# Inverse roots from an exponential of the bits, and new orders on four engines, in the third stage of a decoder kernel

## The reference

```python
x = attn_layer(shift_tokens(x), ...) + x      # second half of the features comes from the token before
x = ffn_layer(shift_tokens(x), ...) + x

# attn_layer: 16 heads of 64
q, k, v = split(x @ Wqkv)
q = l2norm(q) * qs;  k = l2norm(k) * ksc      # l2norm(t) = t / max(norm(t), 1e-12)
q, k = rotary(q), rotary(k)
out = softmax(mask(8 * q @ k.T)) @ v          # keys from 32 tokens back to the token itself
return out @ Wo
# ffn_layer
xn = (x - mean) / sqrt(var + 1e-05) * g + b
a, gate = split(xn @ W1 + b1)
return a * gelu(gate) @ W2 + b2
```

## Time and profile before

| | before |
|---|---|
| median of 3 runs | 3703.31 us |
| the profiled execution's own time | 3706.61 us |
| span of its trace | 3704.8 us |
| PE busy | 3253.5 us, 88% of the span |
| DVE busy | 2801.0 us, 76% |
| ACT busy | 2487.4 us, 67% |
| POOL busy | 2652.6 us, 72% |
| mean granted TensorE clock | 0.986 of full speed |

### The profile page before, as it was taken

How to read it: one execution, slowest core, us unless ns; L and a number is a source line. 1 busy time by engine, 2 the same in 40 slices (tenths; PEclk the granted TensorE clock), 3 DMA queues, 4 the chain that set the end, 5 groups by cost and what they waited for, 6 DMA issues and landing times.

```text
span 3704.8 us, 124977 instructions
## 1 busy us (share of the span) xinstructions
PE 3253.5 (88%) x51333; PEld 2530.0 (68%) x51333; DVE 2801.0 (76%) x5681; ACT 2487.4 (67%) x4952; POOL 2652.6 (72%) x5005
## 2 busy tenths in 40 slices
PE   8999997888888888888888888888888888888886
PEld 6778775666666666666666666766666666666665
DVE  6844446888787888887888878788778878888885
ACT  5756664676666767666667667677666766667664
POOL 5522227877787887787778877777777778777774
PEclk9999999999999999999999999999999999999999
DMA  4000004444445444444444444444444444444442
GB/s 96 3 8 8 8 6 96 102 95 94 87 103 109 92 93 90 100 104 97 94 93 89 101 104 97 90 93 95 103 103 94 95 88 98 94 98 90 97 95 52
DMA packets 280546, 310.50 MB, mean 84 GB/s; under 512 B 154281, under 2 KB 225582, under 8 KB 279982
## 3 DMA queue, kind: packets, MB, share of 16 engines
q0 software_dynamic: 58368, 201.36, 28.0%
q1 hardware_dynamic: 220892, 100.93, 10.7%
q10 hardware_dynamic: 722, 0.21, 0.0%
HBM read 23.63 MB, written 2.10 MB: 7 GB/s over the span
## 4 chain that ended last, share of the span: by engine, by line
PE 59%; DVE 25%; issue 8%; ACT 5%; POOL 1%; SPq 1%; DMA 1%; DVEq 0%; POOLq 0%
PE bank L1153 10%; PE bank L1235 8%; PE bank L1209 8%; PE bank L1123 8%; DVE RK L1403 6%; DVE Z L1459 6%; PE bank L1094 6%; DVE ss L1424 6%; PE bank L1110 4%; PE bank L1134 3%; ACT sq L1300 3%; ACT xnT L1283 2%; PE bank L709 2%; PE bank L722 2%; PE bank L731 2%
## 5 line engine op out<-in xcount | busy, mean ns | idle before, releaser
L1403 DVE TENSOR_TENSOR RK<-bank,tables 128x1024 f32<-128x1024 f32 x384 | 468.7, 1222 | 329.3 <-ACT sq L1300 326.2
L1209 PE MATMUL bank<-xnT,W 128*128 128x128 f32 (+1 forms) x2304 | 322.8, 294 | 350.0 <-DVE Y L1376 349.3
L1389 DVE TENSOR_TENSOR RQ<-bank,q_tables 128x1024 f32<-128x1024 f32 x384 | 452.1, 1219 | 153.3 <-ACT sq L1294 153.2
L1209 PEld LDWEIGHTS bank<-xnT,W 128*128 128x128 f32 (+1 forms) x2304 | 282.6, 190 | 371.0 <-issue 371.0
L1546 POOL TENSOR_TENSOR P<-P,inv_sum 128x512 f32<-128x512 f32 x384 | 505.7, 1634 | 5.7 <-DVE inv_sum L1471 5.7
L1534 POOL TENSOR_TENSOR RK<-RK,rn 128x512 f32<-128x512 f32 x384 | 400.2, 1042 | 28.4 <-POOL rn L1574 0.9
L1520 POOL DMA_DIRECT2D RQ<-RQ x384 | 350.1, 1041 | 97.2 <-DVE RQ L1389 90.2
L1153 PE MATMUL bank<-WA,xcT 128*128 128x512 f32 x768 | 376.8, 613 | 37.0 <-DVE P L1450 16.7
L1540 POOL TENSOR_TENSOR P<-P,rn 128x512 f32<-128x512 f32 x384 | 402.4, 1048 | 3.8 <-DVE P L1450 3.8
L1267 ACT ACTIVATE kT<-bank 128x512 f32<-128x512 f32 x384 | 229.5, 598 | 249.8 <-PE bank L1094 249.8
L1235 PE MATMUL bank<-WO,OT 128*128 128x128 f32 x3072 | 382.3, 278 | 0.0
(11 more groups left out here) (166 smaller groups left out, 7567.4 us busy)
## 6 DMA issues: line engine op xcount, KB each, us to landing
RQ<-RQ POOLq DMA_DIRECT2D x384, 256.0 KB, 4.0
RK<-RK POOLq DMA_DIRECT2D x192, 512.0 KB, 4.7
Z<-Z SPq DMA_DIRECT2D x768, 64.0 KB, 2.5
WA<-in_wqkv SPq DMA_DIRECT2D x24, 256.0 KB, 2.8
ystat<-Y SPq DMA_DIRECT2D x192, 32.0 KB
ystat<-Y SPq DMA_DIRECT2D x384, 15.8 KB
ys<-Y SPq DMA_DIRECT2D x192, 32.0 KB
ys<-Y SPq DMA_DIRECT2D x384, 15.8 KB
```

Of the source, the lines that this page charges most:

```text
L1209: last = mm(FF_BANK[c][0:rows, side * 128:(side + 1) * 128], m.W1[:, off + at:off + at + rows], m.xnT[:, t % 2, :], start=True, stop=True)
L1389: tt(both, src.unsqueeze(1).to_broadcast([128, 2, 8, SEQ]), m.q_tables[:, layer(t), :, :].unsqueeze(2).to_broadcast([128, 2, 8, SEQ]), ALU ...
L1403: tt(both, src.unsqueeze(1).to_broadcast([128, 2, 16, 32]), tab.unsqueeze(2).to_broadcast([128, 2, 16, 32]), ALU.mult).then_inc(s.rotated. ...
```

## The change

The parts of the diff that only rename or resize semaphores and buffers are left out. A column for the variance is added to ssm, seed and rn (32 to 33 wide), so that the seed and the Newton steps work on 33 numbers for a token. The guess comes from one ACT instruction, an exponential of the float's bits read as an integer; two Newton steps follow in place of three, the first with its constants multiplied by 1 + 1.67e-4. The input of the feed-forward part, ys, gets a third buffer. The orders of ACT, DVE, POOL and SP change; PE keeps its order and gets two other waits.

```diff
+SEED_SCALE = -0.5 * math.log(2.0) / 2.0 ** 23
+SEED_BIAS = 0.5 * math.log(2.0) * (127.0 - 0.04303)
+FIRST_STEP = 1.0 + 1.67e-4
...
# SP
         def ff_input(t):
             if exists(t):
                 sp.wait_ge(s.y1, t + 1)
-                at_least(sp, s.xn, t - 1)
-                shifted(m.ys, s.ys[t % 2], t)
+                at_least(sp, s.xn, t - 2)
+                shifted(m.ys, s.ys[t % 2], t, t % 3)
...
         for i in range(N + LAST + 1):
+            ff_input(i - 5)
             layer_input(i + 1)
-            ff_input(i - 5)
...
# PE: keys(t, 1) and keys_turned(t, 1)
+                else:
+                    at_least(pe, s.h, 3 * (t - 7))
...
-                if j == 1 and t == N - 1:
-                    pe.wait_ge(s.y1, t - 3)
+                if j == 1:
+                    at_least(pe, s.y1, t - 3)
...
# ACT
+        def seeded(i):
+
+            if i < N + 5:
+                act.wait_ge(s.q_floor, min(i + 1, N))
+                act.wait_ge(s.k_floor, min(i + 1, N))
+                at_least(act, s.variance, i - 4)
+                nc.scalar.activation(m.seed[:, i % 2, :], m.ssm[:, i % 2, :].bitcast(I32), ACT.Exp, scale=SEED_SCALE,
+                                     bias=m.seed_bias[:, 0:1]).then_inc(s.seed, 1)
...
             squares(i, QUERIES, 1)
+            normalised(i - 6)
             keys_out(i - 1, 1)
             squares(i, KEYS, 1)
...
             query_lengths_out(i)
+            squares(i, KEYS, 0)
             normal_out(i - 6)
-            squares(i, KEYS, 0)
             keys_out(i - 1, 0)
+            exponents(i - 2, 1)
             values_out(i, 1)
-            exponents(i - 2, 1)
             outputs_out(i - 4, 1)
+            values_out(i, 0)
             outputs_out(i - 4, 0)
-            values_out(i, 0)
+            seeded(i)
             exponents(i - 2, 0)
-            normalised(i - 5)
...
# DVE
                 nc.vector.bn_aggr(m.mv[:, t % 2, :], m.stats[:, :]).then_inc(s.var, 1)
+                dve.wait_ge(s.var, t + 1)
+                if t + 5 >= N:
+                    dve.wait_ge(s.lengths, 8 * (t + 4))
+                nc.vector.tensor_scalar(m.ssm[:, (t + 5) % 2, 32:33], m.mv[:, t % 2, 1:2], EPS, None, ALU.add)\
+                    .then_inc(s.variance, 1)
...
-        def seeded(t):          # floor, shift and subtraction
+        def key_floor(t):       # the floor alone
...
             query_rotary(i, 0)
             query_rotary(i, 1)
+            ff_added(i - 8)
+            key_rotary(i, 1)
+            query_floor(i)
+            key_rotary(i, 0)
+            squares_summed(i)
             statistics(i - 5)
-            key_rotary(i, 0)
-            query_floor(i)
-            key_rotary(i, 1)
-            squares_summed(i)
+            key_floor(i)
             probs_turned(i - 3, 1)
             probs_turned(i - 3, 0)
-            ff_added(i - 8)
-            seeded(i)
+            maximum(i - 1, 1)
             maximum(i - 1, 0)
-            row_sums(i - 2, 0)
             less_maximum(i - 1, 0)
             row_sums(i - 2, 1)
-            maximum(i - 1, 1)
+            less_maximum(i - 1, 1)
+            inverse_sums(i - 2, 1)
             attention_added(i - 4)
-            inverse_sums(i - 2, 1)
             gated(i - 7)
-            less_maximum(i - 1, 1)
+            row_sums(i - 2, 0)
             inverse_sums(i - 2, 0)
...
# POOL
-        def inverse_deviation(t):    # three instructions with a power
...
+        def inverse_lengths(i):
+            if i < N + 5:
+                pool.wait_ge(s.seed, i + 1)
...
+                for step, gain in ((0, FIRST_STEP), (1, 1.0)):
...
+        def mean_shift(t):
+            if exists(t):
+                pool.wait_ge(s.lengths, 8 * (t + 6))
+                at_least(pool, s.xn, t - 1)
+                nc.gpsimd.tensor_scalar(m.nmr[:, t % 2:t % 2 + 1], m.mv[:, t % 2, 0:1], m.rn[:, (t + 5) % 4, 32:33], -1.0,
+                                        ALU.mult, ALU.mult).then_inc(s.shift, 1)
...
-            queries_added(i)
             probs_scaled(i - 3, 1)
             probs_scaled(i - 3, 0)
             keys_added(i)
-            inverse_deviation(i - 5)
+            queries_added(i)
             inverse_lengths(i)
+            mean_shift(i - 5)
             keys_scaled(i, 1)
             scores_scaled(i - 1, 0)
             keys_scaled(i, 0)
```

More of the change, by code:

```diff
@@ L18 @@
+import math
 import numpy as np
@@ L135, in build @@
         m.ss = sb("ss", [128, 2, 16])
[L136 to L141, removed]
+        m.ssm = sb("ssm", [128, 2, 33])
+        m.seed = sb("seed", [128, 2, 33])
+        m.seed_bias = sb("seed_bias", [128, 1])
+        m.rn = sb("rn", [128, 4, 33])
+        m.rn_a = sb("rn_a", [128, 33])
+        m.rn_b = sb("rn_b", [128, 33])
         m.RK = sb("RK", [128, 2, 1024])
@@ L154, in build @@
         m.OT = sb("OT", [128, 2, 1024])
-        m.ys = sb("ys", [128, 2, DIM])
+        m.ys = sb("ys", [128, 3, DIM])
         m.stats = sb("stats", [128, 6])
@@ L276, in _ @@
         pool.memset(m.spare[:, :], 0.0)
+        pool.memset(m.seed_bias[:, :], SEED_BIAS)
+        pool.memset(m.ssm[:, :, :], 1.0)
         pool.memset(m.H[:, :, :, :], 1.0)
@@ L989, in local @@
     s.x_turned, s.x_copied = sem("local_x_turned"), sem("local_x_copied")
-    s.qk, s.squared, s.rotated = counted("qk", *four), counted("squared", (QUERIES, 0), (QUERIES, 1), (KEYS, 1), (KEYS, 0)), counted("rotated", *four)
-    s.summed, s.seed, s.lengths = sem("local_summed"), sem("local_seed"), sem("local_lengths")
+    s.qk, s.squared, s.rotated = counted("qk", *four), counted("squared", (QUERIES, 0), (QUERIES, 1), (KEYS, 1), (KEYS, 0)), counted("rotated", (QUERIES, 0), (QUERIES, 1), (KEYS, 1), (KEYS, 0))
+    s.summed, s.k_floor = sem("local_summed"), sem("local_k_floor")
+    s.variance, s.seed, s.lengths = sem("local_variance"), sem("local_seed"), sem("local_lengths")
     s.q_lengths, s.q_lengths_copied = sem("local_q_lengths"), sem("local_q_lengths_copied")
@@ L997, in local @@
     s.v, s.v_copied = counted("v", 1, 0), counted("v_copied", 1, 0)
-    s.scores, s.mx, s.less = sem("local_scores"), counted("mx", 0, 1), counted("less", 0, 1)
-    s.scaled, s.probs, s.row_sum = counted("scaled", 0, 1), counted("probs", 1, 0), counted("row_sum", 0, 1)
+    s.scores, s.mx, s.less = sem("local_scores"), counted("mx", 1, 0), counted("less", 0, 1)
+    s.scaled, s.probs, s.row_sum = counted("scaled", 0, 1), counted("probs", 1, 0), counted("row_sum", 1, 0)
     s.inverse, s.normal = counted("inverse", 1, 0), counted("normal", 1, 0)
@@ L1002, in local @@
     s.o, s.o_copied, s.wo, s.y1 = sem("local_o"), counted("o_copied", 1, 0), sem("local_wo"), sem("local_y1")
-    s.stats, s.var, s.vare, s.pow, s.rstd = (sem("local_stats"), sem("local_var"), sem("local_vare"), sem("local_pow"),
-                                             sem("local_rstd"))
+    s.stats, s.var, s.shift = sem("local_stats"), sem("local_var"), sem("local_shift")
     s.xn, s.xn_turned, s.xn_copied = sem("local_xn"), sem("local_xn_turned"), sem("local_xn_copied")
@@ L1021, in _, with shifted @@
     def _(sp):
-        def shifted(dst, ready, t):
-            y, k = tile_of(m.Y, t), t % 2
+        def shifted(dst, ready, t, k):
+            y = tile_of(m.Y, t)
             sp.dma_start(dst[:, k, 0:64], y[:, 0:64]).then_inc(ready, 16)
@@ L1033, in layer_input @@
                 at_least(sp, s.y, t - TILES + 1)
-                shifted(m.ystat, s.ystat[t % 2], t)
+                shifted(m.ystat, s.ystat[t % 2], t, t % 2)
         def ff_input(t):
@@ L1325, in normalised @@
             if exists(t):
-                act.wait_ge(s.rstd, t + 1)
-                nc.scalar.activation(m.xn[:, t % 2, :], m.ys[:, t % 2, :], ACT.Identity,
-                                     scale=m.rstd[:, t % 2:t % 2 + 1], bias=m.nmr[:, t % 2:t % 2 + 1]).then_inc(s.xn, 1)
+                act.wait_ge(s.shift, t + 1)
+                nc.scalar.activation(m.xn[:, t % 2, :], m.ys[:, t % 3, :], ACT.Identity, scale=m.rn[:, (t + 5) % 4, 32:33],
+                                     bias=m.nmr[:, t % 2:t % 2 + 1]).then_inc(s.xn, 1)
+        def seeded(i):
[5 more added lines that the diff above has]
+                                     bias=m.seed_bias[:, 0:1]).then_inc(s.seed, 1)
         def gates(t):
@@ L1396, in key_rotary @@
                 dve.wait_ge(s.squared.sem, s.squared.upto((KEYS, half), t + 1))
-                if half == 0:
+                if half == 1:
                     at_least(dve, s.k_turned.sem, s.k_turned.upto(0, t))
@@ L1408, in query_floor @@
                 dve.wait_ge(s.q_lengths_turned, t + 1)
+                at_least(dve, s.lengths, 8 * (t - 1))
                 sums = LENGTHS[:, 128:256].rearrange("p (g r) -> p g r", r=32)[:, :, 0:4]
@@ L1416, in statistics @@
                 dve.wait_ge(s.ys[t % 2], 48 * (t // 2) + 48)
-                nc.vector.bn_stats(m.stats[:, :], m.ys[:, t % 2, :]).then_inc(s.stats, 1)
```

(21 more changed lines are left out.)

9 lines of the change are left out of this document (4 added, 5 removed).

## The result

The changed kernel takes 3253.3 us (median of 4 runs, 3251.44 to 3260.95), against 3703.1 us before (median of 4 runs): a ratio of 0.8786, 95% interval 0.8769 to 0.8804. The span of the profiled execution went from 3704.8 to 3249.6 us, 455.2 less.

The account below looks back on a forecast made before the run. No engine was full; a ring in which PE's ff_in waits 1.84 us for DVE's ff_added bound the kernel. Savings of 333, 5 and 8 us (346) took 3706.6 to 3360.6, median 3357 us; range 3330 to 3380, eight in ten 3330 to 3440.

Parts of the forecast that it names:

- PE's work without the wait: On PE: 15.97 us an iteration less the 1.84 us wait at ff_in leaves 14.13 us of work and short gaps.
- The clock: Closing PE's pauses lifts its clock from 0.99; of 14 us for dips and layer changes, 8 come back.
- Filling: In iterations 2 to 8 keys wait for less_maximum; the shorter DVE chain behind keys saves 5 us.
- ff_added moved: On DVE, ff_added behind query_rotary ends near 7.8, wanted by PE at 12.4, so the 1.84 us wait goes.
- The slacks: Spare time before PE would wait: ACT's V 0.3 us, scores 0.6, less_maximum and gated 1.1, transposed keys 2.6.
- POOL's 14.07 us as a bound: POOL worked 14.07 of 15.97 us; without its part of the change, a 14.1 us iteration would hang on it too.
- SP and ys: ff_input's DMAs land by 8.7, statistics stands at 11.5, so the ys wait (59.8 us in 64 waits) goes.
- the chain of 10.6 us: DVE from key_rotary to the end of its iteration takes 10.6 us, 10.43 before, and is not late.
- seeded: New ACT instruction, taken as 0.25 us; ACT ends at about 13.2, is wanted at 14.17, slack 1 us.
- its estimate of 8 us more: In the last iterations, ACT table changes at the skill page's 2.66 us against 1.28 traced: 8 us more, 3365.
- The place of the first: Rival: a small wait remains at ff_in (for values_out) or scores; ACT 0.6 later gives 14.4 us, 3412; chance 0.14.
- The slower one: Rival: the seed ties ACT to the ys transfer; ys landing 3.8 us late gives 16.9 us, 3880; chance 0.05.

Follow-up runs that it names:

- a1: Kernel before, with DVE's less_maximum moved ahead of attention_added and gated, plus the two PE waits this needs: 3631.4 us, ratio 0.9805.
- u2: Changed kernel with DVE's less_maximum late again, behind gated and row_sums: 3450.1 us, ratio 0.9341.
- a2: Kernel before, with DVE's ff_added alone moved behind query_rotary and ff_in waiting for key_rotary itself: 3593.9 us, ratio 0.9712.
- u3: Changed kernel with a third Newton step put back, four more POOL instructions: 3271.2 us, ratio 0.8848.
- a3: Kernel before with both DVE moves, less_maximum early and ff_added early; arithmetic and other engines' orders as before: 3450.9 us, ratio 0.9323.
- a4: a3 plus the keys' order: DVE takes half 1 first, ACT squares half 0 ahead of normal_out: 3405.1 us, ratio 0.9202.
- a5: a4 plus ACT's order: exponents ahead of values_out, values_out(i, 0) ahead of the second outputs_out: 3357.3 us, ratio 0.9069.
- a6: a5 plus DVE's statistics behind squares_summed and SP's ff_input ahead of layer_input; root arithmetic and POOL's order as before: 3321.0 us, ratio 0.8988.
- u4: Changed kernel with SP's order of before (layer_input ahead of ff_input) and two buffers of ys: 3252.3 us, ratio 0.8794.
- u5: Changed kernel with two more DVE reductions an iteration, results unused, behind row_sums: 3292.3 us, ratio 0.8909.

## Why the prediction was wrong in size

- *PE's work without the wait, 15.97 - 1.84 = 14.13 us: wrong, and the step that failed.* The forecast's 14.13 us an iteration was 13.73. The subtraction took every other microsecond of PE's chain for work. The prediction saw that keys and less_maximum "came together" and priced it at nothing. It was a second wait of 0.36 us (a1 removes it, u2 brings it back); another 0.04 lay in ff_in, whose products take 1.52 to 1.53 us in place of 1.57 when they need not wait. 0.40 us in 181 iterations are 72 of the 109 us missed in the span.
- *The clock: direction right, size wrong.* The pauses' dips and the irregular iterations gave back 24.8 us and not 8. The forecast netted 14 us out of a mean that held the shorter filling iterations, so it saw less than half of the 31 us. All of the slow-clock iterations go with the one pause at ff_in (a2). The rule of the Trainium skill (TensorE: Matmul & The Clock Gate, part 1) that activity holds the clock up agrees: 1.00 in both stretches above.
- *Filling, 16 us and not 5,* and 9 us at the two ends, booked as 0. With the third Newton step back (u3) 6.8 of the 16 are lost again, and 6.7 at the end; the rest was not looked into.
- *ff_added moved, 1.84 us: right that the wait goes, wrong that the move is its price.* Alone it takes the chain's iteration from 15.97 to 15.52 us (a2). The other rings stood close behind it: over keys 15.5, over ACT's V 14.7 (a3) and 14.5 (a4), over SP 14.4 in the stretch shown (a5), over gated 14.0 and POOL 13.9 us (a6).
- *The slacks: none failed, but not all had their size.* PE waits for none in the changed kernel. By its rows scores have 0.6 us (forecast 0.6), ACT's V 0.45 (0.3) and less_maximum 0.8 (1.1). gated has 0.28 us and not 1.1: the prediction wanted it when the products of the keys' second half start, but their weight load asks for it 0.8 us earlier than that. And the transposed keys have 1.1 to 1.4 us and not 2.6. Gated's slack held partly by luck: 0.3 us more of DVE ahead of it and by these rows this ring would have set the pace, as it does in a6.

```profile
1800.95 0.86 DVE L1498 SCALAR_TENSOR_TENSOR H<-bank,b1col,G 128x128 f32<-128x128 f32 x3
```

```profile
1802.09 0.19 PEld L1160 LDWEIGHTS bank<-WA,xcT 128*128 128x128 f32 x1 [0.24 <-DVE H L1498]
```

- *POOL's 14.07 us as a bound at 14.1: nearly right.* It takes 13.92 us (a6), which is above the changed kernel's 13.73. *SP and ys: right* (u4).
- *DVE: the chain of 10.6 us was right* within what the rows tell: from key_rotary's start to the end of the last reciprocal of its iteration it is 10.4 us. Against PE's shorter iteration its idle time is 0.8 us, not over 1, and u5 finds it.
- *seeded: 0.32 us and not 0.25,* off the path. In the regular iterations no table load precedes it. In the last ones, which have no exponents, one does (1.28 us, at 3225.20 and 3232.09), as the prediction counted. The further 1.38 us a change, from which its estimate of 8 us more came, is not in the trace: seeded starts 0.02 us after the load ends, and the stretch behind the last query floor got 6.2 us shorter.
- *The rivals:* none came. The place of the first, ACT's V ahead of ff_in, was where a3 and a4 wait. The slower one named ys, which holds a ring in a5; in the changed kernel and in u4, where ACT's seed does hang on statistics, next to nothing waits for ys (in u4 8 times, 3.2 us in 2000).

## What to carry to other kernels

The length of a PE row behind a wait is not PE's pace: where a weight load could not start ahead, the time is counted in the row (1.95 for 1.72 us here), and PE looks busy: 99.7% of the time in a6, at 14.0 us an iteration, and 99.9% in the change, at 13.7. Look at the weight loads' own waits before subtracting a wait from the iteration. Where several rings have nearly one length, price a change as a whole by the longest that is left, and each part by itself only down to the next ring: here the first move alone gave 104 of 450 us. When a loop is brought to its bound, look for the pauses' slow clock as a second gain, and count it from the irregular iterations, not from a mean.

## What the runs showed of the hardware that was not expected

- The DMAs take longer to land in the denser kernel (medians): the two of queries_added 6.8 us (4.0 before), probs_moved 4.6 (2.5), keys_added 5.0 (4.7). Issuing also takes longer: POOL's issue for queries_added has a mean of 1310 ns and had 1041, and SP's for probs_moved, 0.60 to 0.69 us before, takes up to 1.80 us in the iteration shown:

```profile
1811.44 0.69 SPq L1053 DMA_DIRECT2D Z<-Z  x1
1812.17 1.41 SPq L1054 DMA_DIRECT2D Z<-Z  x1
1813.63 1.80 SPq L1053 DMA_DIRECT2D Z<-Z  x1
```

- The POOL instruction right behind a pair of DMA issues is recorded long whatever it is: 1.65 us for the scaling of P before, which takes 1.05 in the new order, and now 0.92 us for the first Newton instruction, 0.24 elsewhere. The record starts before the issue ends (1810.72 against 1811.36), and the length moves with the position; I take it for overlap with the issue and not for work, which no run tried.
